# Moving steps of one batch's side work by a few tiles within a gated attention and expert kernel

## The reference, cut to what matters

```
x = x + tanh(g_xattn) * attention(layernorm(x), ctx, ctx)
    # scores = Q K^T / 4 + adj, masked; softmax; weights V; Wo
x = x + tanh(g_ffn) * experts(layernorm(x))
    # p = softmax(h gate_w^T); e = argmax(p)
    # (relu(h w1[e] + b1[e]) w2[e] + b2[e]) * p[e]
```

## Time and profile before

| | |
|---|---|
| median of 3 runs | 571.88 us (569.12 to 575.5) |
| profiled execution | 572.78 us, of which the profiled span is 570.8 us |
| TensorE busy | 532.1 us, 93% of the span |
| VectorE, ScalarE, GpSimd busy | 298.7, 304.6, 304.2 us (52 to 53%) |
| granted TensorE clock, mean | 0.996 |

### The profile page before, as it was taken

How to read it: one execution, slowest core, us unless ns; L and a number is a source line. 1 busy time by engine, 2 the same in 40 slices (tenths; PEclk the granted TensorE clock), 3 DMA queues, 4 the chain that set the end, 5 groups by cost and what they waited for, 6 DMA issues and landing times.

```text
span 570.8 us, 13582 instructions
## 1 busy us (share of the span) xinstructions
PE 532.1 (93%) x4126; PEld 405.8 (71%) x4127; DVE 298.7 (52%) x908; ACT 304.6 (53%) x675; POOL 304.2 (53%) x461
## 2 busy tenths in 40 slices
PE   7999999989999989999999998879997899999996
PEld 5576666657566657666666765548897899999995
DVE  2676677875577876576876878813510111111111
ACT  4466676666677566678665676443232233333331
POOL 6345476765466665467573646451425445544441
PEclk9999999999999999999999999989999999999999
DMA  8633526301216410105510078778137656555650
GB/s 280 206 107 101 170 87 201 103 20 48 101 39 201 131 41 1 76 18 167 177 49 1 28 247 213 161 258 313 57 37 279 195 166 163 189 196 192 198 186 6
DMA packets 51392, 77.22 MB, mean 135 GB/s; under 512 B 9945, under 2 KB 34601, under 8 KB 51209
## 3 DMA queue, kind: packets, MB, share of 16 engines
q1 hardware_dynamic: 46600, 67.72, 37.2%
q0 software_dynamic: 4096, 8.29, 5.2%
q10 hardware_dynamic: 640, 0.52, 0.3%
HBM read 52.76 MB, written 7.89 MB: 106 GB/s over the span
## 4 chain that ended last, share of the span: by engine, by line
PE 51%; DMA 18%; issue 10%; DVE 7%; POOL 5%; ACT 4%; SPq 4%; POOLq 1%; DVEq 0%; ACTq 0%
PE bank L941 13%; DMA out_y<-cT,sidx 10%; PE bank L953 9%; PE bank L931 7%; PE bank L834 4%; DVE prob L1551 3%; DMA slot_d<-pair,posi 3%; SPq L345 3%; PE bank L1116 2%; PE bank L869 2%; PE bank L915 2%; PE bank L1031 2%; PE bank L1106 2%; ACT pt L1209 2%; POOL rows L739 2%
## 5 line engine op out<-in xcount | busy, mean ns | idle before, releaser
L1551 DVE CUSTOM_DVE_ANT_0 prob<-bank,adjm 128x512 f32<-128x512 f32 x256 | 172.5, 687 | 82.1 <-issue 50.1
L672 POOL TENSOR_SCALAR prob<-prob,negmax 128x512 f32<-128x512 f32 x192 | 133.2, 698 | 130.6 <-DVE negmax L1551 125.7
L1209 ACT ACTIVATE pt<-bank 128x512 f32<-128x512 f32 x256 | 150.3, 594 | 87.6 <-PE bank L941 83.3
L941 PE MATMUL bank<-ident,prob 128*128 128x128 f32 x1024 | 154.8, 274 | 4.6 <-POOL prob L672 2.3
L941 PEld LDWEIGHTS bank<-ident,prob 128*128 128x128 f32 x1024 | 124.2, 141 | 43.5 <-issue 14.7
L1278 ACT ACTIVATE adjm<-bank,colsm 128x128 f32<-128x128 f32 x184 | 52.6, 368 | 107.5 <-PE bank L1106 86.0
L931 PE MATMUL bank<-w2s 128*128 128x512 bf16 x256 | 97.5, 381 | 7.6 <-DVE negmax L1551 4.9
L953 PE MATMUL bank<-pt,vals 128*32 128x256 f32 x1024 | 69.1, 389 | 0.7 <-DVE vals L1365 0.5
L1727 DVE TENSOR_TENSOR cT<-bank,maski 128x256 f32<-128x256 f32 x18 | 7.6, 424 | 117.3 <-PE bank L1116 103.3
L1106 PEld LDWEIGHTS bank<-xT,pt 128*128 128x128 f32 x576 | 67.1, 192 | 1.8 <-ACT xT L1272 1.0
L1106 PE MATMUL bank<-xT,pt 128*128 128x128 f32 x576 | 67.3, 275 | 0.7 <-ACT xT L1272 0.7
(11 more groups left out here) (192 smaller groups left out, 604.0 us busy)
## 6 DMA issues: line engine op xcount, KB each, us to landing
pt<-in_L_ffn_w SPq DMA_DIRECT2D x19, 1024.0 KB, 5.2
w2s<-parts SPq DMA_DIRECT2D x96, 128.0 KB
w2s<-in_L_ffn_w SPq DMA_DIRECT2D x8, 1024.0 KB, 9.9
maski<-in_mask_Bx1xSxS_ik SPq DMA_DIRECT2D x4, 1024.0 KB, 5.4
w2s<-parts SPq DMA_DIRECT2D x56, 64.0 KB, 2.1
xres<-in_x SPq DMA_DIRECT2D x18, 128.0 KB, 2.2
x_d<-rows SPq DMA_DIRECT2D x18, 128.0 KB, 1.7
xn_d<-rows SPq DMA_DIRECT2D x18, 128.0 KB, 2.5
```

What stands on the lines that cost most here:

```text
L672: po.tensor_scalar(prob[:, m], prob[:, m], -1.0, negmax[:, m:m + 1], ALU.mult, ALU.add).then_inc(s_shpool, 1)
L941: mm = pe.transpose(tr_bank[n % NTB][:, c * P:(c + 1) * P], prob[:, n % TILES % NB, c * P:(c + 1) * P], ident[:])
L1209: act.activation(pt[:, g % 2, :, j, q2 * P:(q2 + 1) * P], tr_bank[c % NTB][:].rearrange("p (c q) -> p c q", c=QT), ACT.Exp).then_inc(s_cac ...
L1551: ve.tensor_tensor_reduce(out=prob[:, m % NB], in0=sc_bank[m % NS][:], in1=adjm[:, qt], scale=-1.0, scalar=BIG, op0=ALU.add, op1=ALU.min, ...
```

## The change

Some entries of the lists of steps get other numbers; no instruction is added or taken away. Of the first three batches: the second turn 25 to 26, the gate of two blocks 43 to 44, the first half of k's projection 26 to 27, the last gate 66 to 68. With k's projection go its second matmul, ScalarE's part, VectorE's remainder, GpSimd's cast and split, all one step later. The deviation of x goes from 66 to 67, its normalisations from 67, 69, 71, 73 to 69, 70, 72, 73; the slot writes from 53, 55, 57, 59 to 54, 59, 62, 67 and the wait for them from 72 to 73. In the last batch the third slot write goes from 45 to 46. `TAIL_A` serves the code after the loop too, but there only the order of its entries counts, which stays.

```diff
-    TAIL_A = [(15, "heads", 0), (18, "heads", 1), (23, "turn", 0), (25, "turn", 1), (29, "out", 0),
-              (33, "out", 1), (38, "normed", 0), (41, "normed", 1), (43, "gate", (0, 1)), (51, "rank", 0)]
+    TAIL_A = [(15, "heads", 0), (18, "heads", 1), (23, "turn", 0), (26, "turn", 1), (29, "out", 0),
+              (33, "out", 1), (38, "normed", 0), (41, "normed", 1), (44, "gate", (0, 1)), (51, "rank", 0)]
...
-                     (21, "next q", 0), (26, "next k", 0), (30, "next q", 1), (35, "next k", 1)]
+                     (21, "next q", 0), (27, "next k", 0), (30, "next q", 1), (35, "next k", 1)]
...
-                     (66, "gate", (3,))], key=lambda use: use[0])
+                     (68, "gate", (3,))], key=lambda use: use[0])
...
-    STATS_STEPS, RSTD_STEP, NORM_STEPS = (61, 62, 64, 65), 66, (67, 69, 71, 73)
+    STATS_STEPS, RSTD_STEP, NORM_STEPS = (61, 62, 64, 65), 67, (69, 70, 72, 73)
...
-    SLOT_STEPS, SCATTERED_STEP = ((53, 55, 57, 59), (41, 43, 45, 47)), (72, 60)
+    SLOT_STEPS, SCATTERED_STEP = ((54, 59, 62, 67), (41, 43, 46, 47)), (73, 60)
```

## The result

The changed kernel takes **584.67 us** (median of 4 runs, 582.15 to 586.52) where the one before takes 571.66 beside it (4 runs, 569.12 to 575.5): ratio 1.022, interval 1.0171 to 1.0269. It is slower, as forecast, but by 13.0 us and not by 6.3, and 584.67 lies above the range. The profiled execution took 583.27 with a span of 581.3, so the profiled pair differs by 10.5 us. The mean granted clock of TensorE was 0.985, before 0.996.

What follows compares the result with a forecast made beforehand. It took TensorE, busy 93% of the span, to bound the kernel. Losses of 10.8 less gains made +6.3 us: 579.1 on the profiled 572.78, stated as 578.2; own range 575 to 581.5, over all cases 570.5 to 583.

Steps and rivals of the forecast that it cites:

- The failed step: Sum for the stretch with turn and k's projection: two waits less the turn's gain, 3.59 us a batch, 10.8 in three.
- The two waits: New TensorE waits before q's second half (step 30, 2.31 us) and k's second half (step 35, 1.93 us), each batch.
- The split not late: Rival: GpSimd reaches k's split before VectorE reaches step 33, so the second wait falls away; 572.4 us, chance 0.17.
- the bank free in time: Rival: k's remainder is done before TensorE reaches q's second half, so neither wait appears; 565.4 us, chance 0.10.
- The gains not there: Rival: each removed wait comes back on VectorE or GpSimd, so the loss stands alone; 582.7 us, chance 0.13.
- The turn: Turn 1 moved from 25 to 26: a plain step fills its wait for q's first remainder; gain 0.65 us a batch.
- The gate (0,1): Gate moved from 43 to 44: a plain step fills its wait for turned rows; gain 0.32 us a batch.
- The slot writes: Slot writes 2 to 4 moved to 59, 62, 67: gain 0.57, 0.57 and 0.5 us, 1.64 in all, bounds 0 and 2.
- The rule I weighed there: VectorE two-port tensor_scalar and GpSimd instruction exclude each other; the write at 62 would stop normalisation 63 up to 0.57 us.
- The end of the loop: Deviation, norms and last gate moved, from step 66 on: gain 0.9 us in batches 1 and 2 each, 0.1 in the third.
- The wait for the slot writes at 73: GpSimd's wait moved from 72 to 73, nearer the last write: costs nothing, 1 us a batch if the cover fails.

Runs made afterwards that it cites:

- k alone: The kernel before with only k's first projection moved from 26 to 27: 590.69 us, ratio 1.0264.
- later deviation: The changed kernel with GpSimd's first row deviation moved from step 32 to 33, behind k's split: 580.1 us, ratio 1.0151.
- q later: The changed kernel with q's second projection half moved from step 30 to 31: 571.82 us, ratio 1.0014.
- again: The changed kernel measured once more with no edit: 586.27 us, ratio 1.0194 to the kernel before.
- slot writes alone: The kernel before with only the slot writes and their wait moved as in the change: 570.22 us, ratio 0.9936.
- k back: The changed kernel with k's first projection put back at step 26, other moves kept: 570.65 us, ratio 0.9917.
- kept busy: The changed kernel with 18 unused matmuls ahead of q's second projection half, during the first wait: 582.18 us, ratio 1.0125.

## Why the prediction was wrong in size

*The failed step.* The sum is made of waits alone. "Together this stretch loses 2.31 + 1.93 - 0.65 = 3.59 us a batch" leaves out what TensorE does behind the wait: its granted clock drops to 0.50 for 3.4 us, and steps 31 and 32 cost 1.63 us more, in two loops of the profiled execution and in three of the next one. That is 3.3 to 4.9 us which no term and no bound of the range holds. Keeping TensorE busy took it away and left 1.0125, near the forecast's 1.011. That the rest comes out so near is in part luck: gate and slot writes gained 0.7 us more than forecast, turn and loop's end 1.4 less. The trace before had shown a fall behind a wait once, and I did not use it. TensorE's timeline of the kernel before, behind the attention, and its granted clock there in the columns of the windows:

```profile
380.80 0.41 PE L1019 MATMUL bank<-ident,parts 128*128 128x128 f32 x2 [2.56 <-DMA parts<-xn_d,eidx]
```

```profile
382.11:385.52 3.41, 3.41 (x28) 2.18 (x21) 0.00 (x0) 0.38 (x1) 0.32 (x1) 0.50 0.42 143
```

A wait of 2.56 us, and 1.3 us behind its end the lower level.

*The two waits* were right in place, releaser and size: 2.28 for 2.31 and 1.93 for 1.93, in all three loops. So were their reasons: undoing one entry removes both, moving q's half removes the first, moving the deviation halves the second.

*The split not late* (0.17) is refuted by 172.67 in GpSimd's rows, *the bank free in time* (0.10) by 164.14 in TensorE's. *The gains not there* (0.13) gave 582.7, nearest to what was measured, but by a wrong path: the gains are there. Its sum is off as well: it kept the turn's gain, and with no gain at all the two waits make 3 x 4.24 = 12.7 us, 584.6. That this is the measured time is luck. And the range over all cases left out my own faster case of 565.4.

*The turn* gained 0.50 to 0.52 of 0.65; with k's projection back 0.62 to 0.66, so the term was right, and beside k's move 0.1 of it is lost. *The gate (0,1)* gained 0.47, above its upper bound of 0.32. The idle time that a row shows is less than what the stop costs TensorE: 0.32 shown, 0.47 gained; 1.65 shown, 1.93 lost; 2.01 shown, 2.28 lost. The gate's own eight matmuls, 1.06 behind the wait, take 0.96 without it.

*The slot writes* gained 1.90 over three loops for 1.64. The rule I weighed there, that the write now at 62 would stop the next normalisation, did not come true: in batch 2 the normalisation took 0.41, begun inside that write's record. VectorE and GpSimd of the changed kernel:

```profile
211.93 0.41 DVE L1417 TENSOR_SCALAR rows<-rows,mv,rstd 128x256 f32<-128x256 f32 x1
```

```profile
211.59 1.02 POOL L635 DMA_INDIRECT slot_d<-pair,posi  x1 [0.16 <-issue]
```

By the Trainium skill, "SBUF — State Buffer", section "Who interferes with whom", a normalisation in a two-port mode should have stood until the write was done, as the one of 198.98 before seems to have the earlier trace rows. With the old slot steps (before, k alone) all six such normalisations begin 0.21 or 0.22 us into a write and take 0.98 or 0.99; with the new ones the eight that begin inside the write at 62 begin 0.34 to 0.66 us into it and take 0.41 to 0.48. Spans on GpSimd are rough, and which part of the write holds VectorE up stays open.

*The end of the loop* was too hopeful: 0.9, 0.9 and 0.1 forecast, 0.50, 0.08 and 0.33 measured. I let the norm go later and counted two row minima ahead of it, but left out that GpSimd's own next shifts queue behind write and deviation, and that TensorE's transposes need them. Moving that one write brought 1.38 and 1.13, more than the 0.9 forecast. In the second loop there is also a late hand-on. TensorE and ScalarE of the changed kernel:

```profile
219.41 0.60 PE L941 MATMUL bank<-ident,prob 128*128 128x128 f32 x4
```

```profile
221.24 0.60 ACT L1209 ACTIVATE pt<-bank 128x512 f32<-128x512 f32 x1 [2.19 <-PE bank L941]
```

The transposes end at 220.01, and ScalarE, released by them, starts at 221.24. With the same end of the loop the run with the later deviation shows 10.90 for steps 64 to 74 there instead of 11.31, so some 0.4 of the missing gain belongs to that execution. *The wait for the slot writes at 73* cost nothing that the table shows.

With the measured terms in place of mine the loops lose 6.9 us without the clock (2.0, 2.6 and 2.3) and 10.1 with it.

## What to carry to other kernels

A step moved by one place is not one step later for everything that uses its bank or its buffer: write down the order of uses of each bank and of each in-order queue before and after, and look for the next user that stayed where it was. When a sum of waits on TensorE is made, look what the granted clock does behind each wait of that length; here, where the clock fell, that was another 70% on what the wait cost. A queue's small neighbours (a deviation, a slot write) set when a shared buffer comes free: moving the one was worth 0.99 us a loop, moving the other 0.9 in the first. And when one move takes a wait away, look for what else stands ahead of the same instruction: with q later, the second wait kept its length behind another queue.

## What the runs showed that I had not expected

A TensorE wait of 2.0 us in a kernel that keeps it busy for 93% of the span brought the clock to its lower level, yet not always: in 2, 3, 1 and 1 of the three loops in the four profiled executions that have it (changed kernel, again, k alone, later deviation). None of the 15 second waits of 1.65 to 1.68 us in the executions that have them at full length was followed by a fall. Behind the attention, the wait before L1019 that a fall followed before (2.56 us) is 2.69 us with the slot writes alone and 2.42 with q later, and no fall came for over 40 us. So the length of the wait alone does not decide it, and what does stays open.

A released engine can start late for no reason that the rows show: besides the 1.2 us above, with k back steps 64 to 74 of the second loop took 12.78 us instead of 10.91 as in the first, with a TensorE wait of 2.27 us and a clock fall at 212.97 behind it, which cost 1.50 us more in the first steps of the third loop. No other run shows as much at that place. Smaller losses in the second loop stand in four others: steps 64 to 74 took 0.5 us longer with k alone, and steps 58 to 64 took 8.40, 8.61 and 8.84 us instead of 8.02 (again, kept busy, q later), which takes back two thirds or all of the slot writes' gain there. No experiment looked for their cause.
